# Turning attention's probabilities: one transposing DMA per pair of heads for the second 128 queries, TensorE transposes for the first 128

## The reference

```
q, k, v = x @ wq.T, x @ wk.T, x @ wv.T          # (4, 16 heads, 256, 16)
scores = einsum("bqhd,bkhd->bhqk", q, k), -inf above the diagonal
attn = softmax(scores / 16)
ctx = einsum("bhqk,bkhd->bqhd", attn, v)
out = ctx @ wo.T + b_o
```

## Time and profile before

| | us |
|---|---|
| three runs | 424.41, 421.07, 424.38 (median 424.38) |
| profiled execution | 425.93 |
| its span, first to last instruction | 424.2 |
| PE, DVE, ACT, POOL busy | 386.5, 297.4, 256.7, 236.0 |
| TensorE clock granted, mean | 0.975 of full |

### The profile page before, as it was taken

The page is one execution under the profiler, slowest core; times in us unless marked ns, Lnnn a source line. Parts: engine busy times, 40 slices in busy tenths (PEclk is TensorE's granted clock), DMA queues, the critical chain, the costliest instruction groups (busy, mean ns, idle before and its releaser), DMA issues.

```text
span 424.2 us, 9276 instructions
## 1 busy us (share of the span) xinstructions
PE 386.5 (91%) x2732; PEld 313.3 (74%) x2733; DVE 297.4 (70%) x620; ACT 256.7 (61%) x640; POOL 236.0 (56%) x307
## 2 busy tenths in 40 slices
PE   8879999999999989597898997887899999999996
PEld 4548888888888857366666766564688888888885
DVE  6877999555666797876777586968356775556666
ACT  2736875566555555888897797722355555655553
POOL 5155445565567359557877487200555555654860
PEclk9889999999999999989998898999999999999999
DMA  8949922112111710377757667727741211111126
GB/s 280 371 115 391 378 79 63 52 37 74 49 49 37 257 55 0 75 113 138 121 117 131 96 125 117 130 42 255 224 144 51 63 53 49 62 49 51 48 92 229
DMA packets 71953, 51.57 MB, mean 122 GB/s; under 512 B 54128, under 2 KB 65648, under 8 KB 71664
## 3 DMA queue, kind: packets, MB, share of 16 engines
q1 hardware_dynamic: 67088, 37.00, 33.8%
q0 software_dynamic: 4544, 12.07, 9.3%
q10 hardware_dynamic: 288, 2.10, 1.3%
HBM read 29.37 MB, written 9.19 MB: 91 GB/s over the span
## 4 chain that ended last, share of the span: by engine, by line
PE 66%; DVE 18%; DMA 7%; issue 4%; ACT 3%; POOL 1%; DVEq 0%; SPq 0%; ACTq 0%; POOLq 0%
PE bank L1398 28%; PE bank L1420 14%; PE bank L1570 4%; PE bank L1408 4%; DMA pT<-parts 4%; DVE parts L1204 3%; PE bank L1319 3%; DVE neg_max L1190 3%; PE bank L1374 2%; PE bank L1537 2%; DMA arena<-xn_scratch,gather_row 2%; PE bank L1609 1%; DVE v L1274 1%; PE bank L1340 1%; ACT bank L806 1%
## 5 line engine op out<-in xcount | busy, mean ns | idle before, releaser
L540 POOL DMA_INDIRECT arena<-xn_scratch,gather_row x46 | 49.3, 1071 | 69.4 <-PE bank L1374 47.9
L546 POOL DMA_INDIRECT y_scratch<-arena,scatter_row x42 | 63.0, 1499 | 38.9 <-ACT arena L709 37.7
L1398 PE MATMUL bank<-w_hi,xT_hi 128*128 x184 | 62.4, 421 | 0.0
L1048 DVE TENSOR_TENSOR wo_lo<-w_out,wo_hi 128x1024 fp32r<-128x1024 f32 x46 | 56.4, 1225 | 4.4 <-PE bank L1420 2.3
L1053 DVE TENSOR_TENSOR gT_lo<-bank,gT_hi 128x512 fp32r<-128x512 f32 x46 | 31.7, 690 | 37.7 <-ACT gT_hi L683 37.7
L1398 PE MATMUL bank<-w_hi,xT_lo 128*128 x184 | 58.0, 396 | 0.0
L1398 PE MATMUL bank<-w_lo,xT_hi 128*128 x184 | 57.7, 395 | 0.0
L676 ACT ACTIVATE arena<-bank 128x512 f32<-128x512 f32 x46 | 27.5, 597 | 46.2 <-PE bank L1398 44.9
L621 POOL TENSOR_TENSOR k_head<-k_hi,head_mask 128x256 fp32r<-128x256 f32 x64 | 38.7, 625 | 27.7 <-PE bank L1571 26.0
L1570 PE MATMUL bank<-k_head,xT_hi 128*128 128x256 f32 (+1 forms) x128 | 41.4, 406 | 12.9 <-DVE parts L1204 11.8
L698 ACT ACTIVATE wo_hi<-w_out 128x1024 fp32r x46 | 48.8, 1061 | 5.7 <-issue 3.2
(11 more groups left out here) (193 smaller groups left out, 916.1 us busy)
## 6 DMA issues: line engine op xcount, KB each, us to landing
w_raw<-in_win_t SPq DMA_DIRECT2D x8, 1024.0 KB, 9.4
w_out<-in_wout_t SPq DMA_DIRECT2D x16, 512.0 KB, 10.4
w_out<-y_scratch SPq DMA_DIRECT2D x8, 512.0 KB, 5.0
xn_scratch<-arena ACTq DMA_DIRECT2D x2, 1024.0 KB, 7.1
x<-in_x SPq DMA_DIRECT2D x4, 256.0 KB, 3.4
pT<-parts SPq DMA_TRANSPOSE x64, 3.3
out<-x SPq DMA_DIRECT2D x4, 256.0 KB, 2.2
arena<-xn_scratch,gather_row POOLq DMA_INDIRECT x46
```

The costliest lines, as they stand in the source:

```text
L540: pool.indirect_dma_start(out=xb[j % 2][:, :], out_offset=None, in_=xn_dram, in_offset=bass.IndirectOffsetOnAxis(ap=gather_row[:, j:j + 1] ...
L546: pool.indirect_dma_start(out=y_dram, in_=y[j % 2][:, :], in_offset=None, out_offset=bass.IndirectOffsetOnAxis(ap=scatter_row[:, j:j + 1], ...
L1048: dve.tensor_tensor(wo_lo[:, :, :], w_out[:, bass.ds(e, 1), :, :].rearrange("p o c d -> p (o c) d"), wo_hi[u][:, :, :].bitcast(F32), ALU.s ...
L1398: last = pe.matmul(bank[2 * half + u][:, :], tok[u][:, k, :], wts[:, bass.ds(e, 1), k, half * H:(half + 1) * H], start=(part == 0 and k == ...
```

## The change

The tail is still turned by DMA, the head by PE.

- SP issues one transposing DMA per pair, the tail's 8 tiles. There are three buffers of `parts` and `pT` instead of two; the third pair lies in the space of `v_rest`, which is free after batch 0's values.
- The head's exponentials are written to SBUF (`probs`) instead of over the scores. PE turns them with two fp32 transposes (`turn_head`) into bank 3 or 4; ACT's head copy and DVE's head remainder read that bank and write `head_hi` and `head_lo`, which PE weighs. All head scores go to bank 2, free again after the pair's exponentials.
- In program order: PE turns a head two steps after its scores, behind the tail scores of its step. ACT's head copy moves to the end of its step (`high_head`). DVE's head remainder moves one step on (`low_head`).
- At the end of attention the filler matmuls stand in two steps instead of three, four each instead of six. The first four values use the banks in another order.

```diff
-VBANK = (3, 4, 5, 6, 5, 6, 5, 6)
+VBANK = (6, 4, 5, 3, 5, 6, 5, 6)
...
-WARM_END = 6
+WARM_END = 4
...
+        def buffer_of(g):
+            return g if g < 2 else (g - 2) % 3
+        def last_user(g):
+            return g - 2 if g < 4 else g - 3
...
             def turn_parts(g):
-                u = g % 2
-                for n, (tiles, turned) in enumerate(((slice(0, 8), tail_turned[u]), (slice(8, 12), head_turned[u]))):
-                    sp.wait_ge(low_ready, g * 2 + n + 1)
-                    if g > 1 and n == 0:
-                        sp.wait_ge(pv_done, g * 2 - 2)
-                    sp.dma_start(pT[u][:, tiles, :], parts[u][:, tiles, :].rearrange("p t k -> p (t k)"), transpose=True)\
-                        .then_inc(turned, 16)
+                u = buffer_of(g)
+                sp.wait_ge(low_ready, g + 1)
+                if g > 1 and g != 4:
+                    sp.wait_ge(pv_done, 2 * last_user(g) + 2)
+                sp.dma_start(pT[u][:, :, :], parts[u][:, :, :].rearrange("p t k -> p (t k)"), transpose=True)\
+                    .then_inc(pT_ready[u], 16)
...
                 act.wait_ge(head_max_done, g + 1)
+                reach(act, probsT_done, g - 1)
                 for hh in range(2):
                     h = 2 * p + hh
-                    keys = bank[2 + u][:, P * hh:P * (hh + 1)]
-                    act.activation(keys, keys, ACT.Exp, bias=neg_max[u][:, 0, hh:hh + 1],
+                    act.activation(probs[u][:, hh, :], bank[2][:, P * hh:P * (hh + 1)], ACT.Exp,
+                                   bias=neg_max[u][:, 0, hh:hh + 1],
...
+            def high_head(b, s):
+                g = b * HPAIRS + (s - SLAG - 1)
+                u = g % 2
+                act.wait_ge(probsT_done, g + 1)
+                reach(act, pv_done, g * 2 - 2)
+                act.activation(head_hi[u][:, :, :], bank[3 + u][:, 0:2 * P].rearrange("p (t k) -> p t k", t=2), ACT.Copy,
+                               scale=P_SCALE).then_inc(head_hi_ready, 1)
...
                     if old if s < SLAG + 1 else new:
-                        high(b, s)
+                        high_tail(b, s)
...
+                    if old if s < SLAG + 1 else new:
+                        high_head(b, s)
...
+            def low_head(b, s):
+                g = b * HPAIRS + (s - SLAG - 2)
+                u = g % 2
+                dve.wait_ge(head_hi_ready, g + 1)
+                dve.scalar_tensor_tensor(head_lo[u][:, :, :], bank[3 + u][:, 0:2 * P].rearrange("p (t k) -> p t k", t=2), P_SCALE,
+                                         head_hi[u][:, :, :], ALU.mult, ALU.subtract).then_inc(head_lo_ready, 1)
...
-                    reach(pe, low_ready, g * 2 - 3)
+                    reach(pe, low_ready, g - 1)
...
-                    reach(pe, low_ready, g * 2 - 2)
-                    to = bank[2 + u][:, 0:2 * P].rearrange("p (h k) -> p h k", h=2)
+                    reach(pe, head_probs_ready, g * 2)
+                    to = bank[2][:, 0:2 * P].rearrange("p (h k) -> p h k", h=2)
...
+            def turn_head(b, s):
+                g = b * HPAIRS + (s - SLAG - 2)
+                u = g % 2
+                pe.wait_ge(head_probs_ready, g * 2 + 2)
+                reach(pe, head_lo_ready, g - 1)
+                for hh in range(2):
+                    last = pe.transpose(bank[3 + u][:, hh * P:(hh + 1) * P], probs[u][:, hh, :], ident[:, :])
+                last.then_inc(probsT_done, 1)
...
                     if old if s < SLAG else new:
                         scores(b, s, True)
-                    if not new and s >= SLAG:
-
-                        pe.wait_ge(attn_added, BATCH)
-                        warm(WARM_END, 7)
+                    if old if s < SLAG + 2 else new:
+                        if not old and s == SLAG + 2:
+
+                            pe.wait_ge(v_rest_ready, VALUES[SLAG][1])
+                        turn_head(b, s)
+                        if not new and s >= SLAG:
+
+                            pe.wait_ge(attn_added, BATCH)
+                            warm(WARM_END, 7)
```

More of the change, by code:

```diff
@@ L110, in build @@
             v = room_sb("v", [P, TILES, HEADS, 3 * HD], BF16)
-            v_rest = [room_sb(f"v_rest{u}", [P, HEADS, HD]) for u in range(VSLOTS)]
+            with ExitStack() as inner_room:
+                v_rest = [inner_room.enter_context(nc.sbuf_tensor(f"v_rest{u}", [P, HEADS, HD], F32)) for u in range(VSLOTS)]
+            parts_late = room_sb("parts_late", [P, 2 * 4, P], F16)
+            pT_late = room_sb("pT_late", [P, 2 * 4, P], F16)
             with ExitStack() as inner_room:
@@ L331, in build @@
         tail_probs_ready = sem("tail_probs_ready")
+        probsT_done = sem("probsT_done")
+        head_hi_ready = sem("head_hi_ready")
+        head_lo_ready = sem("head_lo_ready")
         high_ready = sem("high_ready")
         low_ready = sem("low_ready")
-        tail_turned = [sem(f"tail_turned{u}") for u in range(2)]
-        head_turned = [sem(f"head_turned{u}") for u in range(2)]
+        pT_ready = [sem(f"pT_ready{u}") for u in range(3)]
         pv_done = sem("pv_done")
@@ L811, in exps @@
                     h = 2 * p + hh
[L812 to L816 removed]
+                    act.activation(probs[u][:, hh, :], bank[2][:, P * hh:P * (hh + 1)], ACT.Exp,
+                                   bias=neg_max[u][:, 0, hh:hh + 1],
+                                   accum_out=row_sum[:, batch:batch + 1, 0, h:h + 1]).then_inc(head_probs_ready, 1)
@@ L818, in high, with high_tail @@
+            def high_tail(b, s):
                 g = b * HPAIRS + (s - SLAG - 1)
-                u = (s - 1) % 2
-                used = b * (16 * HPAIRS // 2) + (s - SLAG - 1) // 2 * 16
-                reach(act, tail_turned[u], used)
+                if g == 4:
+                    act.wait_ge(v_ready, TILES)
+                elif g > 1:
+                    user = last_user(g)
+                    act.wait_ge(pT_ready[buffer_of(user)], landed(user))
                 act.wait_ge(tail_probs_ready, g * 2 + 2)
-                act.activation(parts[u][:, 0:4, :], bank[u][:, :].rearrange("p (t k) -> p t k", t=4), ACT.Copy,
+                act.activation(parts[buffer_of(g)][:, 0:4, :], bank[g % 2][:, :].rearrange("p (t k) -> p t k", t=4), ACT.Copy,
@@ L1244, in step @@
                     if old if s < SLAG + 1 else new:
-                        low(b, s, True)
+                        low_tail(b, s)
+                    if s in CHUNK_STEP and (old if s < SLAG + 2 else new):
+                        low_head(b, s)
                     if old if s < SLAG else new:
@@ L1249, in step @@
                         chunk(b, CHUNK_STEP.index(s))
-                    if old if s < SLAG + 1 else new:
-                        low(b, s, False)
+                    if s not in CHUNK_STEP and (old if s < SLAG + 2 else new):
+                        low_head(b, s)
                     if not new and s == 0:
@@ L1577, in weigh @@
                 ago = s < SLAG + 3
-                turned = pT[(s - 1) % 2]
-                used = b * (16 * HPAIRS // 2) + ((s - SLAG - 3) // 2 + 1) * 16
-                pe.wait_ge(tail_turned[(s - 1) % 2], used)
-                pe.wait_ge(head_turned[(s - 1) % 2], used)
+                turned = pT[buffer_of(g)]
+                pe.wait_ge(head_lo_ready, g + 1)
+                pe.wait_ge(pT_ready[buffer_of(g)], landed(g))
                 for hh in range(2):
@@ L1584, in weigh @@
                     both, second = slice(2 * HD * h, 2 * HD * (h + 1)), slice(2 * HD * h + HD, 2 * HD * (h + 1))
-                    for i, rest, (qt, kt) in ((8 + hh, 2, (0, 0)), (2 * hh, 4, (1, 0)), (2 * hh + 1, 4, (1, 1))):
-                        rows = v[:, bass.ds(b * 2 + (kt - 2 * ago), 1), h, :]
+                    for qt, kt in ((0, 0), (1, 0), (1, 1)):
+                        high = turned[:, 2 * hh + kt, :] if qt else head_hi[g % 2][:, hh, :]
+                        low = turned[:, 4 + 2 * hh + kt, :] if qt else head_lo[g % 2][:, hh, :]
+                        rows = v[:, b * 2 + (kt - 2 * ago), h, :]
                         to = bank[5 + qt]
-                        pe.matmul(to[:, both], turned[:, i, :], rows[:, :, 0:2 * HD], start=(kt == 0), stop=False)
-                        pe.matmul(to[:, second], turned[:, i, :], rows[:, :, 2 * HD:3 * HD], start=False, stop=False)
-                        last = pe.matmul(to[:, both], turned[:, rest + i, :], rows[:, :, 0:2 * HD], start=False, stop=(kt == qt))
+                        pe.matmul(to[:, both], high, rows[:, 0:2 * HD], start=(kt == 0), stop=False)
+                        pe.matmul(to[:, second], high, rows[:, 2 * HD:3 * HD], start=False, stop=False)
+                        last = pe.matmul(to[:, both], low, rows[:, 0:2 * HD], start=False, stop=(kt == qt))
                     last.then_inc(pv_done, 1)
@@ L1628, in step @@
                         chunk(b, CHUNK_STEP.index(s))
-                    if not old and s == SLAG + 1:
```

(1 more changed line is left out.)

29 lines of the change are left out of this document (14 added, 15 removed).

## The result

The changed kernel takes **430.32 us** (median of 4 runs, 429.35 to 431.81) against 423.17 for the kernel before (4 runs): ratio 1.0169, interval 1.0122 to 1.0217. It is slower by 1.7%. The forecast was 425.5, "within 1%", with a range up to 431.5: the range holds the time, the likeliest case does not, and neither do the forecast's own 423 to 429. The profiled execution took 431.03 us (span 429.3), which is 5.1 more than before's in both. The medians lie 7.15 apart, since the profiled execution of before lay 1.5 us above the slowest of its four runs and that of the change among its own. One later run of the change, of 1292.5 us, was disturbed and is left out, as the ratios leave out runs of the kernel before more than 1.5% above its fastest.

A forecast was written before the change was run, and what follows sets the result against it. Attention was held by ACT's 2.65 us in ordinary steps and late transfers in a few others. Batches +0.6, first batch +1.2, end -0.7 gave +1.1 on 425.93, so 427.0; median 1.5 lower, 425.5 us, range 418.5 to 431.5.

The forecast's parts named there:

- the likeliest case: The forecast itself: median 425.5 us, running from 423 to 429, chance 0.52.
- The ring: Attention's ordinary steps: tail copy, tail remainder, tail scores, turned head, head copy wait in a circle; 3.07 us against ACT's 2.65.
- No buffer breaks this ring: Attention's steps: claim that no buffer frees the circle of waits from tail copy through turned head to next tail copy.
- The special steps: Attention steps 0 and 3, projections: 3.77 us each; 4 and 5, batch summing: 6.97 together; 6, output projection: 3.46.
- Transfers' waits to nothing: Attention batches: waits for turning DMAs costed at nothing; 40 us less SP issue, some 5 us slack against 3.3 to land.
- The falls at 229 and 260 us gone: Half-clock stretches inside attention's batches vanish with PE's waits for transfers; a fall costs 1.1 to 1.6 us.
- The first batch: Attention's first batch: DVE's pace stays, later tail copy and two ring steps about +0.9, half clock up to 0.6; took +1.2.
- The end: Last weighing: last transfer lands earlier, -0.7 us; ten of 18 fillers gone cost nothing, or 1.2 if the clock falls.
- The median: Whole kernel: 427.0 us profiled, less the 1.5 by which before's median lay below its profiled execution, gives 425.5.
- Rival 2: Clock falls at new places: two stay (2.7), one in batch 1 (1.2), one at the end (1.2); 430.6 us, chance 0.25.
- Rival 1: Attention: transfer waits go and the ring is hidden; batches 24.4 us, total 416 us, chance 0.13.

The follow-up runs named there:

- two cuts: Two single edits to the change: PE turns heads at the start of its step, 423.38 us; ACT copies turned heads one step later, 422.52 us.
- the ring cut: The change with PE turning heads first in its step (423.38 us), ACT's head copy one step later (422.52 us), or both (422.94 us); some variants add fillers.
- dummy transposes: Kernel before plus two identity transposes behind each pair's tail scores, into a bank nothing else reads: 426.81 us, ratio 1.0078.
- its ring cut and its fillers kept: The change with PE turning heads at the start of its step and the kernel before's filler matmuls at the end: 421.25 us, ratio 0.9939 to before.
- turned head first: The change with only PE's order altered, turning heads ahead of output projection and tail scores: 423.38 us, ratio 1.0007 to before.

## Why the prediction was right in its parts and short in its sum

- **The ring: right**, in every link, and shown by two cuts. One claim goes too far, "No buffer breaks this ring". A further buffer of `parts` and `pT` does not, but the two banks that the tail scores take by turns are a link of it, and a third was not tried. The Trainium skill's 390 ns per transpose, a figure for bf16 (VectorE: DVE Perf Modes, "The three transpose paths"), would have given 3.63 us; the trace's 3.05 goes with the row's 0.22 for two fp32 ones.
- **The special steps: nearly right.** 3.78 for the second step with projections (3.77 predicted), 6.96 for steps 4 and 5 (6.97), 3.57 for step 6 (3.46); but the first with projections took 3.94 in batches 2 and 3. A batch is 27.35 on the mean instead of 27.18, three +1.1 instead of +0.6.
- **Transfers' waits to nothing: right, for reasons that held only in part.** I put them down to SyncE's queue, 2.5 us of issue per pair against a step of 2.65, and counted on the third buffer as cover. Sixty-four issues cost the batches nothing at a step of 2.55 once there are three buffers; thirty-two with two buffers wait there, and at the ring's 3.05 two are enough. So with three buffers the halved issues, 40 us of SyncE's time, were worth nothing that shows in the batches. With two they may have counted: ScalarE's waits in the batches were 5.0 us with before's 64 issues and 3.0 with 32, each in one profile. That, and what the head's own transfers did in the kernel before, was not separated.
- **The falls at 229 and 260 us gone: right.** No profile with three buffers has one there; with two buffers and the ring cut one came back behind a late transfer. But before with dummy transposes, with two buffers and 64 issues, has none there either, so how often the kernel before has them is open. The 1.1 to 1.6 us for a fall took batch 1 as the measure, but with the ring cut and no fall batches 2 and 3 are mostly longer too, by 0.1 to 0.4.
- **The first batch: mis-sized, +2.3 against +1.2.** Two terms are off, to be read against the earlier trace rows:

```profile
177.81 1.55 DVE L1313 TENSOR_TENSOR v<-v_rest,v 128x256 bf16<-128x256 f32 x2
...
180.71 1.19 PE L1609 MATMUL bank<-k_head,xT_hi 128*128 128x512 f32 x2 [2.13 <-DVE parts L1233]
...
183.03 0.38 ACT L856 ACTIVATE head_hi<-bank 128x256 f16<-128x256 f32 x1 [1.30 <-PE bank L1620]
...
183.31 0.59 ACT L847 ACTIVATE parts<-bank 128x512 f16<-128x512 f32 x1
```

  Before, the first of these was

```profile
177.60 1.26 DVE L1274 TENSOR_TENSOR v<-v_rest,v 128x256 bf16<-128x256 f32 x2
```

  The pace that DVE sets did not stay: two such pairs of additions to v span 1.55 us each, against 1.20 and 1.26, and the tail scores start 0.5 us later, at 180.71. Why is open. The half clock behind TensorE's long wait (2.13 us) was foreseen, but I capped what it does to the ring at 0.6 us. A link of 1.32 becomes 2.32, so the tail copy comes 2.60 us behind these scores and not 1.60; the step there was 1.7 us longer than before (4.79 against 3.08, tail copy to tail copy). Where the stretch lasts, each step pays 1.0. Before has as long a stretch there, but no ring that it could stretch:

```profile
181.40:184.80 3.40, 3.10 (x27) 2.25 (x27) 2.02 (x5) 3.08 (x12) 2.32 (x4) 0.50 1.26 153
```

- **The end: -1.0 up to the last weighing, as forecast (-0.7); the fillers behind it mis-sized.** "I cost that at nothing while the clock holds, and at one fall, 1.2, if not": it did not hold, in any profile with 8 fillers, and the stage behind the last weighing was 2.6 longer here; the kernels with the ring cut put the fillers' worth nearer 2. This and the first batch are most of the miss; in the sum 1.1 became 5.1.
- **The median: the offset did not carry over.** I took 1.5 off because before's median lay so far below its profiled execution; the change's lies 0.7 below its own. The likely reason, not shown, is the two falls in the batches of before's execution: its mean clock was 0.975, where 84 later runs had 0.968 to 0.992, all but five of them above 0.975.
- **The rivals.** Rival 2's time (430.6) is the measured one, but its mechanism only in part: the fall at the end came, two falls in the batches did not stay and none came in batch 1. The range held the time only because it reached up to this rival's, so that part is luck. Rival 1 gave 416 for a hidden ring. With the ring cut and no wait for a transfer the batches reach 25.0 to 25.5 us, not 24.4, and even with the fillers the time is 421.

**What is left of the change.** With its ring cut and its fillers kept it beats both kernels: 421.25 us, 0.6% under before (0.3 to 0.9%) and some 9 us under the change. The gain is small: before's waits for transfers, though real, came in a few steps of a batch, while its ordinary steps already ran at 2.65 us, against 2.66 with the turned head first.

## What to carry to other kernels

When a step moves from a queue to a compute engine, follow the new operand once round through all engines: a copy that closes one engine's step and waits for work queued behind that same step's result makes a ring that more buffers for the transfers did not loosen here, and moving the work earlier on one engine, or the copy one step later on the other, cut it. Test the parts of a bundle alone: here the order was worth 7 to 8 us and the fillers about 2, while halving the issues earned nothing that shows once there were three buffers. Filler matmuls are easy to drop; look at the granted clock in the stage behind them before doing so.

## What the runs showed of the hardware

- A transposing DMA holds SyncE about as long whether it turns 4 tiles or 8: 1.26 against 1.23 us at the median; landing took 2.5 against 3.0 us.
- Two fp32 transposes with what follows them, from tail scores to copy, took 1.32 us at full clock and 2.32 at half: a link of a ring that looked cheap nearly doubles.
- The same program had, in its two profiles, 3.4 and 13.7 us of half clock at 180 us, with spans of 429.3 and 432.1: a single profile of such a kernel does not give the size of that term.
